# A decoder layer on one core: bank order of a hidden layer, place of one small product, and three tiles' last rows moved to GpSimd

## The reference, cut to what matters

```
logits = x2 @ Wg + bg                       # 8 experts
w      = softmax of the top 2 logits, 0 for the other experts
h_e    = relu(x2 @ W1[e] + b1[e])           # 256 hidden values for each expert
mixed  = sum over e of w_e * (h_e @ W2[e] + b2[e])
y3     = mixed + x2
z      = (y3 - mean) * rsqrt(var + eps) * gamma + beta + x2
out    = (z - mean) * rsqrt(var + eps)
```

## Time and profile before

| what | value |
|---|---|
| time, median of 3 runs (lowest to highest) | 242.9 us (242.84 to 243.76) |
| time of the profiled execution | 242.94 us |
| its span, first to last instruction | 241.2 us |
| mean granted TensorE clock | 0.986 |
| PE matmul busy | 217.2 us, 90% |
| DVE busy | 184.7 us, 77% |
| ACT busy | 133.9 us, 56% |
| POOL busy | 109.7 us, 45% |

### The profile page before, as it was taken

How to read it: one execution, slowest core, us unless ns; L and a number is a source line. 1 busy time by engine, 2 the same in 40 slices (tenths; PEclk the granted TensorE clock), 3 DMA queues, 4 the chain that set the end, 5 groups by cost and what they waited for, 6 DMA issues and landing times.

```text
span 241.2 us, 7190 instructions
## 1 busy us (share of the span) xinstructions
PE 217.2 (90%) x2720; PEld 184.3 (76%) x2720; DVE 184.7 (77%) x631; ACT 133.9 (56%) x221; POOL 109.7 (45%) x219
## 2 busy tenths in 40 slices
PE   8889999999999868888899999999999999999920
PEld 6767678777776656668778997789978999689920
DVE  0689999899998988465655578977889679946884
ACT  2588989999999975321588102870059401890000
POOL 5099997989998892244802100260005300221223
PEclk9999999999999999999999999999999999999995
DMA  5920533966566473100000000010000100010001
GB/s 149 291 69 11 104 66 63 141 131 135 109 121 135 106 102 74 30 4 1 3 0 0 3 0 1 0 46 0 4 0 0 45 3 1 0 45 1 0 12 33
DMA packets 32452, 12.29 MB, mean 51 GB/s; under 512 B 19906, under 2 KB 32290, under 8 KB 32418
## 3 DMA queue, kind: packets, MB, share of 16 engines
q1 hardware_dynamic: 31698, 11.54, 23.4%
q10 hardware_dynamic: 720, 0.30, 0.6%
HBM read 6.33 MB, written 1.05 MB: 31 GB/s over the span
## 4 chain that ended last, share of the span: by engine, by line
PE 55%; DVE 24%; issue 9%; POOL 6%; ACT 4%; POOLq 0%; DVEq 0%
PE scoreT_pair L1205 9%; PE bank L1219 7%; PE score_pair L1205 7%; PE scoreT_pair L1219 6%; PE bank L957 5%; DVE x_ext L1612 4%; PE bank L961 4%; DVE rowmax L1271 4%; PE bank L882 3%; PE scoreT_pair L914 2%; PE score_pair L898 2%; PE bank L920 2%; DVE odd_sum L1612 2%; POOL rs L476 2%; ACT early L832 2%
## 5 line engine op out<-in xcount | busy, mean ns | idle before, releaser
L589 POOL TENSOR_TENSOR ve<-mv,table 128x4 f32<-128x4 f32 (+2 forms) x19 | 4.7, 247 | 91.3 <-DVE mv L1624 71.9
L1271 DVE TENSOR_REDUCE rowmax<-score_pair 128x8 f32<-128x1024 f32 x32 | 38.9, 1216 | 3.6 <-PE score_pair L898 2.6
L700 ACT ACTIVATE early<-scoreT_pair 128x1024 f32<-128x1024 f32 x32 | 32.8, 1024 | 5.4 <-PE scoreT_pair L914 5.0
L1219 PE MATMUL bank<-w,early 128*128 128x128 f32 x256 | 30.1, 276 | 0.0
L1219 PE MATMUL scoreT_pair<-w,early 128*128 128x128 f32 x256 | 29.9, 275 | 0.0
L1219 PEld LDWEIGHTS bank<-w,early 128*128 128x128 f32 x256 | 29.5, 192 | 0.4
L1219 PEld LDWEIGHTS scoreT_pair<-w,early 128*128 128x128 f32 x256 | 29.2, 192 | 0.0
L1205 PE MATMUL scoreT_pair<-x2T_part,w_part 128*128 128x512 f32 x96 | 26.2, 403 | 1.4 <-DVE odd_sum L1612 1.4
L957 PE MATMUL bank<-early,v_pad 128*32 128x128 f32 x512 | 26.4, 278 | 0.1
L1205 PE MATMUL score_pair<-x2T_part,w_part 128*128 128x512 f32 x96 | 25.6, 400 | 0.6 <-ACT x2T_part L819 0.6
L961 PE MATMUL bank<-early,head_ones 128*32 128x128 f32 x512 | 25.7, 273 | 0.0
(11 more groups left out here) (193 smaller groups left out, 453.9 us busy)
## 6 DMA issues: line engine op xcount, KB each, us to landing
w<-in_w SPq DMA_DIRECT2D x8, 256.0 KB, 3.3
x_ext<-in_x SPq DMA_DIRECT2D x4, 256.0 KB, 5.5
qT_all<-mT SPq DMA_DIRECT2D x32, 32.0 KB, 2.2
early<-in_xT SPq DMA_DIRECT2D x3, 256.0 KB, 4.4
early<-in_ctxT SPq DMA_DIRECT2D x3, 256.0 KB, 5.3
out<-qkv_all SPq DMA_DIRECT2D x3, 256.0 KB, 2.8
table<-in_tables SPq DMA_DIRECT2D x1, 321.0 KB
out<-qkv_all SPq DMA_DIRECT2D x4, 64.0 KB, 1.6
```

The source lines that it names most:

```text
L700: act.activation(prob[n % 2][:, 2 * u:2 * u + 2, :, :], scoreT_pair[:, :].rearrange("p (i j s) -> p i j s", i=2, j=QUAD), ACT.Exp, scale=S ...
L1219: mm = pe.matmul(expert_bank[k % 4][:, e4 * D:(e4 + 1) * D], hT[:, f, n * P:(n + 1) * P], w2[:, f, :], start=(c == 0), stop=(c == CH - 1))
L1271: dve.tensor_reduce(rowmax[:, H // 2 * u:H // 2 * (u + 1)], score_pair[:, :].rearrange("p (r t) -> p r t", t=S), AX_X, ALU.max).then_inc(s ...
```

## The change

Three parts. The first chunks of a group alternate between banks 0 and 1 (chunks 0 to 3), and only chunks 4 and 5 use banks 2 and 3; the waits follow. The b2 mix moves to behind chunk 1 (from behind chunk 2) in groups 1 to 3, and to behind chunk 11 (from behind chunk 8) in group 0, where the gate's transpose moves from behind chunk 7 to behind chunk 8. In the last group, yn, z and the result of tiles 0, 1 and 2 are computed by POOL (yn in two operations, with its own rounding order), while DVE keeps the statistics of z and all of tile 3.

```
-        hidden_bank = bank[0:4]
+        hidden_bank = [bank[i] for i in (0, 1, 0, 1, 2, 3, 0, 1, 2, 3, 0, 1, 2, 3, 0, 1)]
-        LOGITS_AT, GAP_AT, GATE_AT, MIX_AT, NEXT_MIX_AT = 2, 4, 8, 9, 3
+        LOGITS_AT, GAP_AT, GATE_AT, MIX_AT, NEXT_MIX_AT = 2, 4, 9, 12, 2
...
 # SP, store
+                if g == G - 1 and tiles.start == GT - 1:
+                    sp.wait_ge(s["last_res"], 1)
+                else:
+                    sp.wait_ge(s["res_ready"], GT * g + tiles.stop)
...
 # POOL, last group
+            def last_row(n):
+                g = G - 1
+                pool.tensor_scalar(yn[:, n, :], acc[:, g, n, :], mv3[:, n, 0:1], rs3[:, n:n + 1], ALU.subtract, ALU.mult).then_inc(s["last_yn"], 1)
+                pool.wait_ge(s["last_yn"], 2 * n + 1)
+                pool.tensor_tensor(yn[:, n, :], yn[:, n, :], bias[:, GAMMA, :], ALU.mult).then_inc(s["last_yn"], 1)
+                pool.wait_ge(s["last_yn"], 2 * n + 2)
+                pool.tensor_tensor(z[:, n, :], yn[:, n, :], x2b[:, g, n * D:(n + 1) * D], ALU.add).then_inc(s["last_z"], 1)
+            def last_result(n):
+                pool.wait_ge(s["rs4_ready"], G + n)
+                pool.tensor_scalar(res[:, G - 1, n, :], z[:, n, :], mv4[:, n, 0:1], rs4[:, n:n + 1], ALU.subtract, ALU.mult)\
+                    .then_inc(s["res_ready"], 1)
             rows3(0)
+            last_row(0)
             rows3(1)
+            last_row(1)
             rows4(0)
+            last_result(0)
             rows3(2)
+            last_row(2)
             rows4(1)
+            last_result(1)
             rows3(3)
             rows4(2)
+            last_result(2)
             rows4(3)
...
 # ACT and PE, hidden
-                    act.activation(hT[:, c, :], hidden_bank[c % 4][:, :], ACT.Relu, bias=b1[:, c:c + 1])\
+                    act.activation(hT[:, c, :], hidden_bank[c][:, :], ACT.Relu, bias=b1[:, c:c + 1])\
-                    if c >= 4:
+                    if c >= 6:
                         pe.wait_ge(s["hT_ready"], NCH * g + c - 3)
+                    elif c >= 4:
+                        wait(pe, s["summed"], 4 * (2 * GT * g + c - 5))
                     elif c >= 2:
-                        wait(pe, s["summed"], 4 * (2 * GT * g + c - 3))
+                        pe.wait_ge(s["hT_ready"], NCH * g + c - 1)
                     else:
                         wait(pe, s["hT_ready"], NCH * g)
...
 # DVE, last group
+            def last_statistics(n):
+                dve.wait_ge(s["last_z"], n + 1)
+                dve.bn_stats(st4[:, n, :], z[:, n, :]).then_inc(s["z_stats"], 1)
+                dve.wait_ge(s["z_stats"], GT * (G - 1) + n + 1)
+                apart(dve)
+                dve.bn_aggr(mv4[:, n, :], st4[:, n, :]).then_inc(s["z_aggr"], 1)
...
             gather(G - 1, 1)
-            last_sums(0)
+            last_statistics(0)
             weigh(G - 1, 2)
             gather(G - 1, 2)
-            last_results(0)
-            last_sums(1)
+            last_statistics(1)
             weigh(G - 1, 3)
             gather(G - 1, 3)
-            last_sums(2)
-            last_sums(3)
-            last_results(1)
-            last_results(2)
-            last_results(3)
+            last_statistics(2)
+            dve.wait_ge(s["y3_aggr"], GT * G)
+            dve.wait_ge(s["x2b_ready"], G)
+            last_row(GT - 1)
```

More of the change, by code:

```diff
@@ L228, in build_program @@
             logit_ready route gap_ready egap_ready gate_ready gate_tr gateT_ready b2_mixed acc_ready
-            hidden hT_ready experts summed added gate_split b2_high b2_low gate_w_high gate_w_low stored
+            hidden hT_ready experts summed added gate_split last_yn last_z last_res b2_high b2_low gate_w_high gate_w_low stored
             y3_stats y3_aggr ve3_ready rs3_ready yn_ready z_ready z_stats z_aggr ve4_ready rs4_ready
@@ L382, in store @@
             def store(g, tiles):
-                sp.wait_ge(s["res_ready"], GT * g + tiles.stop)
+                if g == G - 1 and tiles.start == GT - 1:
+                    sp.wait_ge(s["last_res"], 1)
+                else:
+                    sp.wait_ge(s["res_ready"], GT * g + tiles.stop)
                 sp.dma_start(out[g * GT + tiles.start:g * GT + tiles.stop].rearrange("n s d -> s n d"), res[:, g, tiles, :])\
@@ L643, in rows4 @@
                 rsqrt4(G - 1 + n, GT * (G - 1) + n + 1, slice(n, n + 1))
+            def last_row(n):
[9 more added lines that the diff above has]
+                    .then_inc(s["res_ready"], 1)
             rows3(0)
+            pool.wait_ge(s["rs3_ready"], G)
+            last_row(0)
             rows3(1)
+            pool.wait_ge(s["rs3_ready"], G + 1)
+            last_row(1)
             rows4(0)
+            last_result(0)
             rows3(2)
+            pool.wait_ge(s["rs3_ready"], G + 2)
+            last_row(2)
             rows4(1)
+            last_result(1)
             rows3(3)
             rows4(2)
+            last_result(2)
             rows4(3)
@@ L1204, in hidden @@
                             pe.wait_ge(s["x2T_low"], g + 2)
-                        mm = pe.matmul(hidden_bank[c % 4][:, :], w1_part[:, w, c * P:(c + 1) * P], x2T_part[:, x, :],
+                        mm = pe.matmul(hidden_bank[c][:, :], w1_part[:, w, c * P:(c + 1) * P], x2T_part[:, x, :],
                                        start=(k == 0), stop=(k == 2))
@@ L1679, in _, with last_row @@
                 tail(g)
[L1681 to L1685, removed]
+            def last_statistics(n):
[4 more added lines that the diff above has]
+                dve.bn_aggr(mv4[:, n, :], st4[:, n, :]).then_inc(s["z_aggr"], 1)
+            def last_row(n):
+                done = GT * (G - 1)
+                dve.scalar_tensor_tensor(yn[:, n, :], acc[:, G - 1, n, :], mv3[:, n, 0:1], bias[:, GAMMA, :],
+                                         ALU.subtract, ALU.mult).then_inc(s["yn_ready"], 1)
+                dve.wait_ge(s["rs3_ready"], G + n)
+                dve.wait_ge(s["yn_ready"], done + 1)
+                dve.scalar_tensor_tensor(z[:, n, :], yn[:, n, :], rs3[:, n:n + 1], x2b[:, G - 1, n * D:(n + 1) * D],
+                                         ALU.mult, ALU.add).then_inc(s["z_ready"], 1)
+                dve.wait_ge(s["z_ready"], done + 1)
+                dve.bn_stats(st4[:, n, :], z[:, n, :]).then_inc(s["z_stats"], 1)
+                dve.wait_ge(s["z_stats"], done + n + 1)
+                apart(dve)
+                dve.bn_aggr(mv4[:, n, :], st4[:, n, :]).then_inc(s["z_aggr"], 1)
+                dve.wait_ge(s["rs4_ready"], G + n)
+                dve.tensor_scalar(res[:, G - 1, n, :], z[:, n, :], mv4[:, n, 0:1], rs4[:, n:n + 1],
+                                  ALU.subtract, ALU.mult).then_inc(s["last_res"], 1)
             start_acc(G - 1)
```

## The result

The changed kernel takes 239.15 us (median; 238.81 to 239.96) against 243.33 us for the kernel before (242.84 to 245.04), both over four runs. The ratio is 0.9856, with a 95% interval of 0.9825 to 0.9888: faster by 1.4%, some 3.5 us (the two medians alone are 4.2 apart). The direction is the one forecast and 239.15 lies in the range, but the forecast was 238.0, a gain of 4.96, so the gain is about 0.7 of it. The profiled execution took 238.96 us.

The account below looks back on a forecast made before the run. The prediction took PE to set the pace in the stages, with waits at their start, and a chain of small dependent operations to set the end. Gains 2.12 + 0.44 + 2.4 = 4.96 off 242.9 gave 238.0; range 237.0 to 239.8.

Parts of the forecast that it names:

- Banks and mix, groups 1 to 3: Group boundaries: PE no longer waits for DVE, the mix covers the relu; gain 0.86 and twice 0.63, sum 2.12.
- DVE next in line: Before group 1's first weighing: DVE's idle time shrinks from 1.15 to 0.29, so it is late next.
- (b): Rival: the boundaries give half, as DVE becomes the bound or relus are late; 239.1 to 239.6, chance 0.07.
- (d): Rival: the bank order saves nothing since PE only waits elsewhere; 240.1, chance 0.02.
- Group 0: First group: later mix avoids the wait for the gate's copy, gain 0.44; DVE begins 0.53 late and catches up.
- The last rows: Tail after PE's last product: moving three tiles' rows to POOL gains 2.4, from 1.0 to DVE's bound of 2.85.
- The working's list of 10.6: Tail: POOL's operations from 225.63 to the last deviation, 7 pairs, 4 two-input operations, 5 tensor_scalar, without idle time.
- The prediction's own sign of being wrong: Tail: tensor_scalar rows of 0.6 or more on POOL; also stretched DVE sums or no DVE idle before first weighing.
- rival (a): The tail gives half or less through dearer POOL operations or holds; each tensor_scalar dearer by 0.2 costs 1.0; chance 0.15.
- Holding: Tail: elementwise work on POOL holds DVE's two-input sums and the reverse; 0.2 taken for edges, 0.9 at most.
- rival c: Slower overall: tensor_scalar on POOL is of another kind, from about 1.4 us for one; chance 0.03.
- The pause: Tail: about 6 us before POOL's first call of a freshly loaded kernel, time near 242.9; chance 0.03.

Follow-up runs that it names:

- e3: The changed kernel with the b2 mix and the gate's transpose back at their old places, banks and tail new; ratio to the kernel before 0.9906.
- e1: The kernel before with only the new bank order, waits and places of mix and transpose, last rows still on DVE; ratio 0.9881.
- e5: The kernel before with scratch operations on POOL where it is idle, to price tensor_scalar against tensor_tensor; 242.44 us in one execution.
- e7: The changed kernel with POOL's six tensor_scalar of the last group replaced by tensor_tensor of the same width, results not correct; ratio to before 0.9765.
- e8: The changed kernel with one more tensor_scalar on POOL between tile 1's result and tile 3's deviation; 241.3 us in one execution.
- e6: Against e4: DVE weighs and gathers tile 3 before the statistics of tiles 1 and 2, POOL takes their deviations together; ratio to before 0.9828.
- e4: The changed kernel with the results of tiles 0, 1 and 2 given back to DVE, computed where it waits; ratio to before 0.9793.

## Why the prediction was partly right and where it failed

**Banks and mix, groups 1 to 3** (forecast 0.86 and twice 0.63, sum 2.12): 0.83, 0.62 and 0.65, from the gate's transpose to the first product, sum 2.10. The mechanism is right, and so is the sum, but its terms fit partly by luck: the mix takes 0.24 and not 0.33, and the hand-over from ACT 0.05 and not 0.14, so next to nothing is left of the wait of 0.08; against that chunks 2 and 3 take 1.52 instead of 1.40, since the wait keeps weight loads from running ahead (one of the working's bounds names this, at 0.2), and chunks 0 and 1 take 1.47 (146.26 to 147.73) instead of 1.40. Forecast from chunk 0 to chunk 4 were 3.21, measured are 3.23. That the mix is the cover was right in kind, and e3 gives it 0.22.

**DVE next in line** (0.29 left): 0.33 left in group 1. Rivals (b) and (d) fall by e1, which has the whole 2.54.

**Group 0** (forecast 0.44, `start_acc` 1.66 later, DVE 0.53 late and catching up): 0.44. DVE's first weighing comes without idle time and it has caught up by the next half, as forecast. The mix begins at 127.58 and `start_acc` at 128.01, where the working has 128.5 and 129.0, less the 1.0 by which this run is ahead.

**The last rows** (forecast 2.4 of a possible 2.85): 0.45. The step that failed is a term of the sum, the price of `tensor_scalar` on POOL: taken as 0.40, between a copy and a two-input sum of the earlier trace rows, it is 0.80 (after, e5). Neither row bounded it; the working took two rows of other kinds of operation for bounds. The path held: five of them on it, POOL full from tile 1's aggregate on, `last_result(2)` ahead of the last deviation. The working's list of 10.6 took 12.41 (222.39 to 234.80). Of the 1.8 more, the five `tensor_scalar` with their hand-overs make 1.67, holds 0.19 and the seven pairs 0.16, and the four two-input operations give back 0.21. The list also began 0.30 later than in the working: 0.21 by the held sum, 0.09 by the hand-over from the aggregate, which the working left out. Together 2.1, and 2.6 less 2.1 is about the 0.45 measured. e7 shows it from one side (near the assumed price the gain is 2.67), e8 from the other (one more operation costs its full length). The prediction's own sign of being wrong, rows of 0.6 or more, appeared. This is rival (a), with the sensitivity it named, 1.0 for each 0.2; it had 0.15 and deserved more, since the list had no slack and the price no row.

**Holding** (0.2, at most 0.9): 0.40 of it reaches the end. The sum at 221.04 gives 0.21, since POOL waits for the aggregate behind it; POOL's own list gives 0.14 at 230.58 and 0.05 at 225.15, where an addition takes 0.24 instead of 0.19 beside DVE's second sum. The third sum, at 228.77, takes 0.54 and costs nothing, since POOL comes to tile 3's aggregate only at 231.49. So this term was too small by 0.2, within its bound. e6 loses 0.27 by a held sum. On the lock for a whole instruction that the Trainium skill's page "SBUF — State Buffer" states in its section "SBUF: two separate sides": the trace after agrees for elementwise work (0.50 and 0.94). For the power it doesn't: in e4 DVE's yn at 231.35, with two SBUF inputs, takes its ordinary 0.35 inside POOL's power of 231.27 to 231.82. The other way round there is a small effect: in e7 the power at 225.10 takes 0.63 instead of 0.55 beside DVE's sum of 225.02.

**Slower** (rival c): its threshold of 1.4 us for one operation was 0.6 away. The pause that the page "GPSIMD Engine Reference" of the Trainium skill gives in section 2.1 for the first call of a freshly loaded kernel did not occur in front of the first `tensor_scalar` (e5, 0.10 behind its predecessor).

**The time.** The two stretches gave 2.99 us. Taken off the forecast's base of 242.9 that is 239.9, just above the range's upper end of 239.8. That the median of 239.15 lies inside the range is thus luck in part: in the profiled pair another 1.0 lies ahead of the first mark.

## What to carry to other kernels

Before work goes to a second engine, add up that engine's list over the stretch: where it comes out full, the price of every operation counts several times over, and one without a row of its own kind should be measured first, in a place where the engine is idle. Put results that nobody waits for on the engine that is waiting (e4), not on the one that is waited for. And move a stall's cover with it: the two alternating banks cost only 0.12 us a boundary because the mix fills the relu's time; without it they cost 0.22 more (e3).

## What the runs showed of the hardware that was not expected

On POOL, a `tensor_scalar` of one tensor is slower than a `tensor_tensor` of two at both widths where both were tried (0.58 against 0.32 at 64 columns, 0.80 against 0.46 at 128), with constants too (0.65 at 128), and grows by about 3.3 ns a column. The time ahead of the feed-forward part varied by 1.8 us over executions of the same instructions; in the profiled pair DVE is 0.42 to 0.48 ahead from its first operations behind the loads on, and 0.5 more from one of its row maxima near 88 us on. e5_prices, which is the kernel before up to there, is ahead of it by the same 0.48 and 0.5 at the same places, so this is no effect of the change. What differs from run to run stays open.

A DVE sum held by POOL goes on before the end that the profile gives for POOL's operation: the sum at 221.04 ends at 221.54 and needs 0.29, so it goes on at 221.25, and POOL's z ends at 221.39. By the same subtraction, an estimate, the sum goes on 0.13 to 0.15 ahead of that end in four other places too (after at 224.96 and 228.77, e4 at 221.78, e6 at 229.40).
